# Tiled small matmuls, a turned softmax divisor, and written-out step orders in a decoder layer

## The chip, the core and the metric

The kernel runs on one core of one Trainium2 chip. A core has TensorE (PE in the profile; PEld is its weight load), VectorE (DVE), ScalarE (ACT), GpSimd (POOL) and SyncE (SP, which here only starts DMAs). The metric is the device time of one execution in microseconds. Every engine works through its own instructions in order and waits on semaphores for the others.

## The reference

A decoder layer on 32 rows of 256 tokens with 256 features, all in float32. Three parts, each on a layer norm of `x` and added to `x`:

```python
# part a: gated linear attention, 4 heads, 64 slots
q, k, v = silu(conv4(x @ Wq)), silu(conv4(x @ Wk)), silu(conv4(x @ Wv)); q, k = rope(q, k)
s = clip(x @ Ws, -32, 32); z = cumlogsumexp(s)        # over the tokens
# hk = hk * exp(z_prev - z) + k (x) exp(s - z); ok = q . hk; qv = softmax(ok)
# hv = hv * exp(z_prev - z) + exp(s - z) (x) v; o = qv . hv
x = x + (rmsnorm(o) * gnorm * silu(x @ Wg)) @ Wo
# part x: cross attention to 77 context tokens, 16 heads of 16
Q, K, V = x @ W_q.T, ctx @ W_k.T, ctx @ W_v.T
x = x + (softmax(where(mask, Q K^T / 4, -1e10)) @ V) @ W_proj.T + b_proj
# part f: 8 experts of 64, the best two by x @ gate_w
x = x + sum over the two of softmax(top2) * ((silu(x @ Wu[e]) * (x @ Wv[e])) @ Wo[e])
```

## The kernel before

**Rows and parts.** Each of the 32 rows goes through four stages, one stage an iteration, so four rows are in work at once: `N` (norm and projections of part a, row i), `A` (its attention, row i-1), `X` (cross attention, row i-2), `F` (experts, row i-3). `iterations` runs `body` B + 3 = 35 times; in the first three and the last three some stages are missing and their steps are simply left out. On each engine `body` is one written-out list of steps, and the list is the order in which the engine works. After iteration 0 every engine also runs `others`, in which the second lot of weights is split; PE waits there for all of the splits.

**Precision.** A matrix that needs float32 accuracy is held as two `fp32r` halves and multiplied three times (`mm_halves`). Operands in plain float32 (`AT`, `E`, `vtok`, `q_bd`, `ET`, `probT`, `Vbd`, and all transposes) are multiplied directly, and the profile shows two MATMULs and two LDWEIGHTS for each such call.

**The three places that the change touches in the matmuls.** `a_A` gives k^T q for all four heads at once: `q_bd` holds q of each head in its own 32 partitions and zeros elsewhere, 4 x 256 columns. `a_P` does the same with `qn_bd` (two heads of 64 partitions each, zeros elsewhere). Both use the whole 128 x 128 array, with products by zero in it. `x_av` multiplies the turned probabilities `probT` (stationary, 128 tokens) with the values `Vbd` (moving): for each of 10 tiles of keys and each of two halves of the row, 34 or 51 columns: 16 values and a one per head. The column of ones gives the sum of the exponentials, `x_rs` takes its reciprocal on VectorE, `x_o` multiplies, and `x_ot` turns the result for the projection `x_proj`.

**Scores.** `x_s(u)`, u = 0 to 7, writes four heads' scores into bank X0; `x_soft(u)` (DVE) takes the row maximum, `x_prob(u)` (ACT, four ACTIVATEs) the exponentials; `x_s(u+1)` waits for `x_prob(u)`, since there is one bank. `x_pt(u)` turns two or three tiles of them (PE, then ACT). Bank X0 is also that of `x_turn`, `x_q` and `x_proj`, so row r+1 starts its part x only after `x_out(r)`.

**Context.** K and V of all rows come from 20 matmul groups `g_mm` in iterations 0 to 2, go to memory and come back row by row (`x_kin`, `x_vbd`). `x_kbd` on POOL spreads K over the heads with zeros: four pieces `K_bd` and two of `KT_lo_bd`, all behind the last scores of the row before.

## Time and profile before

| | us |
|---|---|
| median of 3 runs | 1520.54 (1518.21 to 1521.38) |
| profiled execution | 1518.72 |
| its span on the core | 1516.6 |
| PE busy | 1456.9, 96% |
| DVE, ACT, POOL busy | 1217.1, 961.4, 828.6 |

The span is the time from the first to the last instruction; the execution's own time is 2.1 us longer. A busy PE is not PE at its peak: its matmuls overlap, and an entry's length includes the way through the array. What a matmul costs is therefore read from the distance between the starts of two neighbours, not from its length.

### The profile page before, as it was taken

To read this page: it belongs to the slowest core of one execution; us is meant where nothing else is said; L and a number is where in the kernel's file an instruction comes from. 1 tells how busy PE (TensorE), PEld (TensorE's weight loads), DVE (VectorE), ACT (ScalarE), POOL (GpSimd) and SP (SyncE) were. 2 spreads that over 40 slices of the span, in tenths; PEclk is the share of its full clock that TensorE was granted. 3 is DMA by queue.
4 is the path that set the end of the run, shared out by engine and by line. 5 is a ranking of instruction groups with operands and counts; after the bars stand their busy time and mean duration, and the time that the engine had idled before them with its cause. 6 is when DMAs were issued, how large, how long until landed. Compare 5 with 4: busy or idle time off the path is not lost.

```text
span 1516.6 us, 31405 instructions
## 1 busy us (share of the span) xinstructions
PE 1456.9 (96%) x10520; PEld 1291.4 (85%) x10520; DVE 1217.1 (80%) x3006; ACT 961.4 (63%) x2531; POOL 828.6 (55%) x937
## 2 busy tenths in 40 slices
PE   5798999999999999999999999999999999999975
...
DMA packets 113102, 45.03 MB, mean 30 GB/s; under 512 B 86192, under 2 KB 109104, under 8 KB 112944
## 3 DMA queue, kind: packets, MB, share of 16 engines
...
q14 instruction: 72, 0.59, 0.1%
...
## 4 chain that ended last, share of the span: by engine, by line
PE 91%; DVE 3%; issue 2%; POOL 1%; ACT 1%; DMA 1%; SPq 0%; POOLq 0%; DVEq 0%; ACTq 0%
PE bank L444 76%; PE bank L450 7%; PE bank L685 5%; PE bank L770 2%; PE bank L532 1%; DVE a_conv L887 1%; PE bank L738 0%; DVE a_rC L909 0%; ACT x_prob L1331 0%; SPq L433 0%; DMA x_prob<-in_ctxT 0%; DVE x_nmax L1013 0%; DMA x<-in_x 0%; PE bank L541 0%; DVE x L1035 0%
## 5 line engine op out<-in xcount | busy, mean ns | idle before, releaser
L1331 ACT ACTIVATE x_prob<-bank,x_nmax 128x77 f32<-128x77 f32 x1024 | 248.5, 329 | 51.2 <-DVE x_nmax L1013 50.2
L1013 DVE TENSOR_REDUCE x_nmax<-bank 128x4 f32<-128x308 f32 x256 | 120.1, 469 | 109.8 <-PE bank L444 106.0
L1344 ACT ACTIVATE x_probT<-bank 128x256 f32<-128x256 f32 (+1 forms) x256 | 112.2, 438 | 98.3 <-PE bank L685 98.1
L1497 POOL TENSOR_TENSOR a_orinv<-a_ove,mhalf 128x8 f32<-128x8 f32 x32 | 65.1, 2035 | 199.1 <-DVE a_ove L952 199.1
L444 PE MATMUL bank<-x_Vbd,x_probT 128*128 128x34 f32 (+1 forms) x1280 | 162.5, 267 | 0.7 <-DVE x_o L1027 0.7
L887 DVE SCALAR_TENSOR_TENSOR a_conv<-a_raw,cw,a_conv 128x256 f32<-128x256 f32 x384 | 155.0, 478 | 7.5 <-POOL a_conv L1459 7.5
L444 PEld LDWEIGHTS bank<-x_Vbd,x_probT 128*128 128x128 f32 x1280 | 158.0, 192 | 1.1 <-DVE x_o L1027 1.1
L685 PE MATMUL bank<-ident,x_prob 128*128 128x128 f32 x640 | 114.6, 277 | 0.4 <-ACT x_prob L1331 0.3
L909 DVE RECIPROCAL a_rC<-bank 128x512 f32<-128x512 f32 x32 | 107.1, 3348 | 0.6 <-PE bank L444 0.6
L912 DVE TENSOR_TENSOR a_AT<-bank,tri 128x512 f32<-128x512 f32 x128 | 87.7, 685 | 23.9 <-PE bank L444 23.9
L444 PE MATMUL bank<-x_K_bd,x_Q_stack 128*128 128x308 f32 x256 | 94.5, 369 | 8.6 <-ACT x_prob L1331 5.2
L685 PEld LDWEIGHTS bank<-ident,x_prob 128*128 128x128 f32 x640 | 79.5, 145 | 21.9 <-ACT x_prob L1331 9.7
L1450 POOL TENSOR_SCALAR a_E<-a_E 128x512 f32<-128x512 f32 x32 | 62.1, 1940 | 54.9 <-ACT a_E L1230 54.9
L1459 POOL TENSOR_SCALAR a_conv<-a_raw,cw 128x256 f32<-128x256 f32 x128 | 59.1, 479 | 56.3 <-ACT a_raw L1224 56.3
L1535 POOL TENSOR_TENSOR f_s<-f_s,f_wt 128x512 f32<-128x512 f32 x64 | 66.7, 1043 | 39.0 <-DVE f_wt L1098 25.0
L1349 ACT ACTIVATE x_oT_hi<-bank 128x512 fp32r<-128x512 f32 x32 | 19.2, 598 | 107.2 <-PE bank L450 107.2
L1510 POOL TENSOR_TENSOR x_K_bd<-x_K_stack,groupmask 128x308 fp32r<-128x308 f32 x128 | 86.0, 704 | 0.0
L1434 POOL TENSOR_TENSOR x_rstd<-x_ve,mhalf 128x2 f32<-128x2 f32 x32 | 22.9, 715 | 114.6 <-DVE x_neg L842 114.6
L444 PE MATMUL bank<-x_negmask,ident_bf 128*128 128x308 bf16 x256 | 79.6, 311 | 0.0
L444 PE MATMUL bank<-x_KT_lo_bd,x_Q_stack 128*128 128x308 f32 x256 | 77.4, 302 | 0.0
L1513 POOL TENSOR_TENSOR x_KT_lo_bd<-x_KT_lo,headmask 128x616 fp32r<-128x616 f32 x64 | 76.8, 1221 | 0.0
L444 PE MATMUL bank<-fwo_hi,f_sT_hi 128*128 128x256 f32 x256 | 75.2, 294 | 1.5 <-ACT f_sT_hi L1378 1.5
...
## 6 DMA issues: line engine op xcount, KB each, us to landing
...
x_Vbd<-v_tok SPq DMA_DIRECT2D x128, 9.6 KB
```

Source lines behind the costliest of these rows:

```text
L444: return pe.matmul(out, lhsT, rhs, start=start, stop=stop, skip_group_check=True)
L450: ins = pe.transpose(dst[:, k * T + c * P:k * T + (c + 1) * P], src[:, c, k * P:(k + 1) * P], ident[:])
L685: ins = pe.transpose(X1[:, i * P:(i + 1) * P], prob[:, t * P:(t + 1) * P], ident[:])
L887: stt(conv[:, j, :], raw[:, j, i:i + T], cw[:, j, i:i + 1], conv[:, j, :], ALU.mult, ALU.add).then_inc(on.a_conv, 1)
L909: dve.reciprocal(flat(rC[r % 2]), E0[:, :]).then_inc(on.a_rC, 1)
L912: return tt(dst, src.rearrange("p (h t) -> p h t", h=H), tri.rearrange("p (o t) -> p o t", o=1).broadcast_to([P, H, P]), ALU.mult)
L1013: dve.tensor_reduce(nmax[:, u % 2, :], X0[:, 0:UH * S2].rearrange("p (h s) -> p h s", h=UH), AX.X, ALU.min).then_inc(on.x_max, 1)
L1331: ins = act.activation(prob[:, col:col + S2], X0[:, i * S2:(i + 1) * S2], ACT.Exp, scale=-1.0, bias=nmax[:, u % 2, i:i + 1])
L1344: act.activation(probT[:, g[0]:g[-1] + 1, :].rearrange("p h t -> p (h t)"), X1[:, 0:len(g) * P], ACT.Copy).then_inc(on.x_pT, 1)
L1510: pool.tensor_tensor(K_bd[:, q], K_stack[r % 2][:, q:q + 1, :].broadcast_to([P, UH, S2]), spread(groupmask[:], S2), ALU.mult)
L1513: ins = pool.tensor_tensor(KT_lo_bd[:, f], KT_lo[r % 2][:, f:f + 1, :].broadcast_to([P, HB, S2]), spread(headmask[:], S2), ALU.mult)
L1535: pool.tensor_tensor(fs[:, c, :].rearrange("p (e q) -> p e q", e=NE), fs[:, c, :].rearrange("p (e q) -> p e q", e=NE), spread(wt[:, c, :], ...
```

## The change

**Matmul tiles.** `a_A` and `a_P` now multiply 64 partitions at a time (row tiles 0 to 63 and 64 to 127), one tile into bank A0, the other into A1, each with only its own heads. `qn_bd` and `qn_last` become one plain tile `qnT`, filled by one ACTIVATE in place of three; `q_bd` keeps two column blocks in place of four. In `x_av` the sides are swapped: `Vbd` is stationary with 64 columns (four heads of 16), `probT` moves with 256 columns (both halves of the row), and two column tiles write partitions 0 to 63 and 64 to 127 of bank X2. So part x comes out turned already, 12 calls a row in place of 20.

**The divisor.** The ones in `Vbd` are gone. `x_prob` has each exponential give its sum too (`accum_out`, 32 a row). `x_rs` inverts the sums, a new POOL step `x_rse` spreads them over 16 features (two of 128 x 256 a row), `x_rt` turns that (four transposes, where `x_ot` had four), ACT copies it to `rsT`, and `x_on` multiplies on DVE. `x_ot` on ACT copies from `xo` in place of a bank. `x_prob` also waits for `x_rs` of the row before.

**Orders.** `iterations` calls `first()`, `body(i)` for i = 3 to 31, and `last()`: three lists per engine. `x_kbd`, `a_conv`, `a_rc` (the reciprocal of 128 x 512, now two of 128 x 256) and `f_yy` are cut into single steps that the lists place. The splits of the weights are steps (`w_hi_`, `w_lo_`) in `first()`, and each user waits for its own weight only. `Vbd` is zeroed by POOL and no longer loaded.

```diff
@@ PE @@
-            def a_A(r, c):
-                if c == 0:
-                    ...
-                mm((A0 if c == 0 else A1)[:, :], qkr[r % 2][:, 1, c * P:(c + 1) * P],
-                   q_bd[r % 2][:, :, c * P:(c + 1) * P]).then_inc(on.a_A_ps, 1)
+            def a_A(r):
+                ...
+                for c in range(TC):
+                    for i in range(2):
+                        rows = slice(i * P // 2, (i + 1) * P // 2)
+                        ins = mm((A0 if i == 0 else A1)[:, c * D:(c + 1) * D], qkr[r % 2][rows, 1, c * P:(c + 1) * P],
+                                 q_bd[r % 2][rows, :, c * P:(c + 1) * P])
+            def a_P(r):
+                pe.wait_ge(on.a_qnT, upto(r))
+                for c in range(TC):
+                    for f in range(2):
+                        for i in range(2):
+                            rows = slice(i * P // 2, (i + 1) * P // 2)
+                            ins = mm((A1 if i == 0 else A0)[:, c * D + f * P:c * D + (f + 1) * P],
+                                     ET[r % 2][rows, f, c * P:(c + 1) * P], qnT[rows, f, c * P:(c + 1) * P])
+            def x_av(r, g):
+                ...
+                pe.wait_ge(on.x_pT, upto(r, NU, QU + 2 * (g + 1)))
+                for j in range(VS // 2):
+                    for i in range(2):
+                        t = g * NT // 2 + 2 * i + j
+                        ins = mm(X2[i * VW:(i + 1) * VW, g * T:(g + 1) * T], Vbd[r % 2][:, g, i * VS // 2 + j, :],
+                                 probT[:, t, :], start=(j == 0), stop=(j == VS // 2 - 1))
+            def x_rt(r):
+                pe.wait_ge(on.x_rse, upto(r, TC))
+                pe.wait_ge(on.x_pT, upto(r, NU))
+                ...
+                        ins = pe.transpose(X1[:, f * T + c * P:f * T + (c + 1) * P],
+                                           rse[:, c, f * P:(f + 1) * P], ident[:])
@@ DVE @@
-            def x_rs(r, c):
-                dve.wait_ge(on.x_av_ps, upto(r, NU, (c + 1) * QU))
-                ...
-                tt(xo[:, c, :].rearrange("p (h e) -> p h e", h=NH), src[:, :, 0:HD],
-                        spread(xrs[:, c, :], HD), ALU.mult).then_inc(on.x_o, 1)
+            def x_rs(r, c):
+                dve.wait_ge(on.x_prob, upto(r, NU, (c + 1) * QU))
+                ...
+            def x_on(r):
+                dve.wait_ge(on.x_av_ps, upto(r, 2))
+                dve.wait_ge(on.x_rT, upto(r))
+                ...
+                tt(flat(xo), X2[:, :], flat(rsT), ALU.mult).then_inc(on.x_on, 1)
@@ ACT @@
-                                         bias=nmax[:, u % 2, i:i + 1])
+                                         bias=nmax[:, u % 2, i:i + 1], accum_out=xsum[:, c, q * UH + i:q * UH + i + 1])
@@ POOL @@
+            def x_rse(r, c):
+                ...
+                pool.tensor_scalar(rse[:, c, :].rearrange("p (h e) -> p h e", h=NH), spread(xrs[:, c, :], HD),
+                                   1.0, 1.0, ALU.mult, ALU.mult).then_inc(on.x_rse, 1)
@@ orders, PE's list of the body, a line of each @@
-                N(g_mm, 3); X(x_pt, 0); X(x_s, 1); F(f_lg); N(a_v); A(a_qt); X(x_s, 2); F(f_v0); N(a_s)
-                X(x_av, 6); X(x_av, 7); N(a_et); A(a_wo); X(x_ot); F(f_yy); X(x_proj)
+                x_proj(i - 3); a_vtok(i - 1); a_A(i - 1); g_mm(i, 0); x_turn(i - 2); a_state(i - 1)
+                x_pt(i - 2, 0); a_P(i - 1); x_pt(i - 2, 1); x_s(i - 2, 4); x_pt(i - 2, 2); a_o(i - 1)
```

**PE in the middle of the body, before**, from `x_s(3)` on (`x_K_bd`, `x_KT_lo_bd`, `x_negmask` are the three matmuls of a score step, `ident,x_prob` is `x_pt`):

```order
L444 MATMUL bank<-x_K_bd,x_Q_stack 128x308
L444 MATMUL bank<-x_KT_lo_bd,x_Q_stack 128x308
L444 MATMUL bank<-x_negmask,ident_bf 128x308
L444 MATMUL bank<-a_qn_bd,a_ET 128x256 x4
L685 MATMUL bank<-ident,x_prob 128x128 x3
L444 MATMUL bank<-x_Vbd,x_probT 128x34
L444 MATMUL bank<-x_Vbd,x_probT 128x51
L444 MATMUL bank<-x_K_bd,x_Q_stack 128x308
L444 MATMUL bank<-x_KT_lo_bd,x_Q_stack 128x308
L444 MATMUL bank<-x_negmask,ident_bf 128x308
L685 MATMUL bank<-ident,x_prob 128x128 x2
```

The same place after:

```order
L425 MATMUL bank<-x_K_bd,x_Q_stack 128x308
L425 MATMUL bank<-x_KT_lo_bd,x_Q_stack 128x308
L425 MATMUL bank<-x_negmask,ident_bf 128x308
L693 MATMUL bank<-ident,x_prob 128x128 x2
L425 MATMUL bank<-a_qnT,a_ET 128x128 x8
L693 MATMUL bank<-ident,x_prob 128x128 x3
L425 MATMUL bank<-x_K_bd,x_Q_stack 128x308
L425 MATMUL bank<-x_KT_lo_bd,x_Q_stack 128x308
L425 MATMUL bank<-x_negmask,ident_bf 128x308
```

`a_P` (the `a_qn_bd` row, now `a_qnT` with 128 columns) stands between two turns of the probabilities, and no value matmul stands between the score steps any more.

**PE at the end of the body, before** (`ident,f_s` is `f_st(1)`):

```order
L770 MATMUL bank<-ident,f_s 128x128 x4
L685 MATMUL bank<-ident,x_prob 128x128 x3
L444 MATMUL bank<-x_Vbd,x_probT 128x34
L444 MATMUL bank<-x_Vbd,x_probT 128x51
L444 MATMUL bank<-x_Vbd,x_probT 128x34 x2
L444 MATMUL bank<-x_Vbd,x_probT 128x51
L444 MATMUL bank<-x_Vbd,x_probT 128x34
L444 MATMUL bank<-x_Vbd,x_probT 128x51
L444 MATMUL bank<-x_Vbd,x_probT 128x34
L450 MATMUL bank<-ident,a_E 128x128 x4
```

After:

```order
L693 MATMUL bank<-ident,x_prob 128x128 x3
L431 MATMUL bank<-ident,a_o 128x128 x4
L793 MATMUL bank<-ident,f_s 128x128 x4
L425 MATMUL bank<-x_probT,x_Vbd 64x256 x6
L716 MATMUL bank<-ident,x_rse 128x128 x4
L425 MATMUL bank<-wo_hi,a_oT_hi 128x256
```

The row that read 34 and 51 columns is now 6 calls of 256 columns with 64 results each; the first six stand ahead of `a_c`. The turn of the divisor follows.

**DVE at the start of the run, before** (`wo_lo` to `fwo_lo` are the splits of the second lot of weights):

```order
L995 TENSOR_TENSOR f_sT_lo<-bank,f_sT_hi 128x512 x2
L909 RECIPROCAL a_rC<-bank 128x512
L903 SCALAR_TENSOR_TENSOR a_qkv<-a_qkv,a_conv 128x512
L1158 TENSOR_SCALAR x_o<-a_o,gnorm 128x512
L1153 TENSOR_TENSOR wo_lo<-x_o,wo_hi 128x512
L1153 TENSOR_TENSOR xwq_lo<-x_0,xwq_hi 128x512
L1153 TENSOR_TENSOR xwp_lo<-x_1,xwp_hi 128x512
L1153 TENSOR_TENSOR fgate<-f_topf,fgate 128x2x8
L1153 TENSOR_TENSOR fwu_lo<-f_s,fwu_hi 128x512 x2
L1153 TENSOR_TENSOR fwv_lo<-a_E,fwv_hi 128x512
```

After:

```order
L935 SCALAR_TENSOR_TENSOR a_conv<-a_raw,cw,a_conv 128x256 x6
L898 TENSOR_SCALAR a_okn<-a_o,gnorm 128x512
L857 BN_STATS a_stats<-x_1 128x6 x2
L906 TENSOR_TENSOR wo_lo<-a_okn,wo_hi 128x512
L863 BN_AGGR a_mv<-a_stats 128x2 x2
L935 SCALAR_TENSOR_TENSOR a_conv<-a_raw,cw,a_conv 128x256 x6
L941 SCALAR_TENSOR_TENSOR a_qkv<-a_qkv,a_conv 128x512
L926 SCALAR_TENSOR_TENSOR a_gate<-a_gate,bank 128x512
L946 STREAM_SHUFFLE a_conv<-a_qkv 128x512
```

The convolution is cut in two by the step that needs the second lot of weights, and the splits that stood in one piece behind `a_rC` are spread over three rows' steps.

**PE's first rows, before**, where K of the context came first:

```order
L444 MATMUL bank<-x_prob,xwk 128x512 x4
L444 MATMUL bank<-xwv,x_prob 128x256 x4
L450 MATMUL bank<-ident,a_xn 128x128 x4
L444 MATMUL bank<-a_xnT_hi,wqk_hi 128x256
```

After:

```order
L431 MATMUL bank<-ident,a_xn 128x128 x4
L425 MATMUL bank<-a_xnT_hi,wqk_hi 128x256
L425 MATMUL bank<-a_xnT_lo,wqk_hi 128x256
L425 MATMUL bank<-a_xnT_hi,wqk_lo 128x256
L425 MATMUL bank<-a_xnT_hi,wqk_hi 128x256
```

Row 0's transpose and projections are first, and the context waits behind them.

## Rows read from the trace of the kernel before

**Rows 1.** The page's busy line and the sum of its chain that ended last.
```profile
PE 1456.9 (96%) x10520; PEld 1291.4 (85%) x10520; DVE 1217.1 (80%) x3006; ACT 961.4 (63%) x2531; POOL 828.6 (55%) x937
...
PE 91%; DVE 3%; issue 2%; POOL 1%; ACT 1%; DMA 1%; SPq 0%; POOLq 0%; DVEq 0%; ACTq 0%
```

**Rows 2.** Busy us in three stretches: PE, PEld, DVE, ACT, POOL, then clock, DMA.
```profile
0.00:134.00 134.00, 102.43 (x585) 79.45 (x586) 80.29 (x161) 64.14 (x143) 54.01 (x63) 0.97 0.42 129
134.00:1405.00 1271.00, 1270.07 (x9426) 1141.20 (x9425) 1084.43 (x2697) 852.71 (x2264) 746.77 (x842) 1.00 0.09 21
1405.00:1516.60 111.60, 84.37 (x514) 70.70 (x512) 52.38 (x148) 44.55 (x126) 27.82 (x33) 0.88 0.05 13
```

**Rows 3.** The four transposes that open each iteration, from the third on.
```profile
L532 PE MATMUL bank<-ident,a_qkv x120: 270/272/273, 134.0 to 1405.4; 128*128 128x128 f32 x120
```

**Rows 4.** PE in order of time: start us, us, line, out<-in, shapes.
```profile
704.71 1.02 PE L444 MATMUL bank<-a_q_bd,a_qkr 128*128 128x512 f32 x2
705.57 0.60 PE L450 MATMUL bank<-ident,x_xn 128*128 128x128 f32 x4
...
722.84 1.89 PE L444 MATMUL bank<-a_qn_bd,a_ET 128*128 128x256 f32 x8
724.57 0.49 PE L685 MATMUL bank<-ident,x_prob 128*128 128x128 f32 x3
...
739.70 1.87 PE L444 MATMUL bank<-x_Vbd,x_probT 128*128 128x34 f32 x16
741.40 0.64 PE L450 MATMUL bank<-ident,a_E 128*128 128x128 f32 x4
```

**Rows 5.** Weight loads by form: count, busy us and mean ns.
```profile
L444 PEld LDWEIGHTS bank<-f_xnT_hi,fgate 128*16 128x16 f32 x64 | 6.6, 104 | 2.6 <-ACT f_xnT_hi L1354 1.8
...
L738 PEld LDWEIGHTS bank<-ident,f_lgT 16*128 16x128 f32 x64 | 6.3, 135 | 4.9 <-issue 0.6
```

**Rows 6.** PE timeline around the two tile forms that there are.
```profile
714.06 0.30 PE L444 MATMUL bank<-x_KT_lo_bd,x_Q_stack 128*128 128x308 f32 x1
714.20 0.31 PE L444 MATMUL bank<-x_negmask,ident_bf 128*128 128x308 bf16 x1
...
714.46 0.28 PE L444 MATMUL bank<-f_xnT_lo,fgate 128*16 128x256 f32 x1
714.58 0.28 PE L444 MATMUL bank<-f_xnT_hi,fgate 128*16 128x256 f32 x1
...
716.80 0.31 PE L444 MATMUL bank<-x_negmask,ident_bf 128*128 128x308 bf16 x1
...
717.26 0.39 PE L444 MATMUL bank<-a_xnT_hi,wv_hi 128*128 128x256 f32 x1
717.48 0.28 PE L444 MATMUL bank<-a_xnT_lo,wv_hi 128*128 128x256 f32 x1
```

**Rows 7.** ScalarE timeline: four exponentials, and the smallest ACTIVATE.
```profile
717.66 0.97 ACT L1331 ACTIVATE x_prob<-bank,x_nmax 128x77 f32<-128x77 f32 x4 [0.24 <-DVE x_nmax L1013]
718.50 0.22 ACT L1364 ACTIVATE f_egap<-f_gap 128x2 f32<-128x2 f32 x1
```

**Rows 8.** Chain that ended last: one round of scores of the last row.
```profile
1460.84 0.71 PE bank L444 x3
...
1463.11 0.70 PE bank L444 x3
```

**Rows 9.** Start of the run: the first split of a weight on ScalarE.
```profile
L1409 ACT ACTIVATE wqk_hi<-a_AT x1: 629/629/629, 10.0 to 10.0; 128x512 fp32r<-128x512 f32 x1
```

**Rows 10.** PE timeline at the start, with the idle time before an entry.
```profile
13.55 6.19 PE L444 MATMUL bank<-x_prob,xwk 128*128 128x512 f32 x8 [13.55 <-DMA x_prob<-in_ctxT]
...
50.02 1.09 PE L532 MATMUL bank<-ident,a_qkv 128*128 128x128 f32 x4 [6.78 <-DVE fwo_lo L1153]
```

**Rows 11.** Chain that ended last, at the end of the run.
```profile
1448.34 2.64 POOL x_K_bd L1510 x4
```

**Rows 12.** PE timeline at the end.
```profile
1453.58 0.59 PE L444 MATMUL bank<-x_K_bd,x_Q_stack 128*128 128x308 f32 x1 [2.22 <-POOL x_KT_lo_bd L1513]
```

More of the change, by code:

```diff
@@ L140, in build @@
         qkr = [sb(f"a_qkr_{i}", [P, 2, T]) for i in range(2)]
-        q_bd = [sb(f"a_q_bd_{i}", [P, H, T]) for i in range(2)]
+        q_bd = [sb(f"a_q_bd_{i}", [P, 2, T]) for i in range(2)]
         ktok = sb("a_ktok", [P, P])
@@ L275, in build, with iterations @@
         KV_OUT = 16 * 4
-        def row(i):
-            return i if 0 <= i < B else None
-        def iterations(body, others):
-            for i in range(B + 3):
-                body(row(i), row(i - 1), row(i - 2), row(i - 3))
-                if i == 0:
-                    others()
+        def iterations(first, body, last):
+            first()
+            for i in range(3, B):
+                body(i)
+            last()
         block = ctx.enter_context(nc.Block())
@@ L809, in others @@
[L809 to L819 removed]
+                mm_halves(F0[:, c * D:(c + 1) * D], [
+                    (lambda h, i=i: fsT[h][:, c, i, :], lambda h, i=i: fwo[h][:, i, :]) for i in range(RC)]
+                    ).then_inc(on.f_y_ps, 1)
@@ new lines, in first @@
+            def first():
+                a_turn(0); a_qk(0); g_mm(0, 0); a_v(0); g_mm(0, 1); g_mm(0, 2); a_s(0); g_mm(0, 3)
+                a_g(0); g_mm(0, 4); g_mm(0, 5); g_mm(0, 6); a_c(0); g_mm(0, 7); g_mm(1, 0); a_ktok(0)
+                a_et(0); a_A(0); a_vtok(0); g_mm(1, 1); a_state(0); a_turn(1); a_ok(0); a_qk(1)
+                g_mm(1, 2); a_v(1); a_qt(0); a_P(0); a_s(1); a_o(0); g_mm(1, 3); a_g(1); g_mm(1, 4)
+                g_mm(1, 5); a_ot(0); g_mm(1, 6); a_wo(0); a_c(1); g_mm(1, 7); g_mm(2, 0); g_mm(2, 1)
+                x_turn(0); g_mm(2, 2); a_et(1); a_ktok(1); a_vtok(1); a_A(1); x_q(0); a_turn(2)
+                g_mm(2, 3); a_qk(2); x_s(0, 0); a_state(1); a_v(2); x_pt(0, 0); x_s(0, 1); a_ok(1)
+                x_s(0, 2); x_pt(0, 1); a_s(2); x_pt(0, 2); x_s(0, 3); a_qt(1); x_s(0, 4); x_pt(0, 3)
+                a_P(1); a_g(2); x_s(0, 5); a_o(1); x_s(0, 6); x_pt(0, 4); x_pt(0, 5); a_c(2); x_s(0, 7)
+                x_pt(0, 6); x_av(0, 0); x_pt(0, 7); a_ot(1); x_av(0, 1); x_rt(0); a_wo(1); a_et(2)
+                a_ktok(2)
@@ L822, in _ @@
+            iterations(first, body, last)
         @block.vector
@@ L1166, in _ @@
             dve.tensor_copy(ones_r[:], ones[:])
-            dve.wait_ge(ld_w, W_LANDED)
-            dve.tensor_copy(tri_r[:], tri_raw).then_inc(w_ready, 1)
-            dve.tensor_copy(ident_bf[:], ident[:]).then_inc(w_ready, 1)
-            split(splits, 0)
-            dve.wait_ge(w_ready, 4)
-            iterations(body, others)
+            iterations(first, body, last)
         @block.scalar
@@ L1422, in _ @@
+            iterations(first, body, last)
         @block.gpsimd
@@ L1562, in _ @@
                 pool.memset(q_bd[i][:], 0.0).then_inc(z_ready, 1)
-            pool.memset(qn_bd[:], 0.0).then_inc(z_ready, 1)
-            def others():
-                pool.wait_ge(ld_v, V_LANDED)
-                pool.wait_ge(on.g_ps, 4)
-                pool.memset(prob[:], 0.0).then_inc(z_ready, 1)
-                pool.wait_ge(z_ready, 4)
-            pool.wait_ge(ld_w, W_LANDED)
-            pool.wait_ge(w_ready, 4)
-            iterations(body, others)
+            for i in range(2):
+                pool.memset(Vbd[i][:], 0.0).then_inc(v_zero, 1)
+            iterations(first, body, last)
 def constants():
```

602 lines of the change are left out of this document (348 added, 254 removed).

## Prediction, made before the run

> **What bounds the kernel now.** I read the page's sums first, then the chain that ended last, then busy time by stretch, then PE's timeline inside one iteration. The sums show PE busy for 96% of the span and 91% of the chain on PE [rows 1]. The stretches show where that holds: from 134 to 1405 us PE is busy 1270.07 of 1271.00 us at full clock, while DVE has 1084.43, ACT 852.71 and POOL 746.77 us of it [rows 2]. The first 134 us have 102.4 us of PE and the last 111.6 us have 84.4 [rows 2]. So the middle is bound by what PE issues, the two ends by dependencies. The transposes that open an iteration start at 134.0 for iteration 3 and at about 1405.1 for iteration 32 (the last of four is at 1405.4) [rows 3]: 29 iterations in 1271.1 us, 43.83 us each. Per iteration DVE has 1084.43 / 29 = 37.4, ACT 29.4 and POOL 25.8 us. The span is 134.0 + 1271.1 + 111.5 = 1516.6 us.
>
> **x_av.** A row has 20 calls before, that is 40 matmul passes (float32 takes two). Sixteen of them run from 739.70 to 741.40, 106 ns each [rows 4], though they have only 34 or 51 columns: the load of 128 weight columns sets that pace. 40 x 0.106 = 4.25 us. After there are 12 calls, 24 passes of 256 columns. Eight passes of 256 columns take 722.84 to 724.57, 0.216 us each [rows 4]. One after the other that is 5.19 us, 0.94 more than before. If the two column tiles always ran beside each other it would be half, 2.60. As written, each call's two passes come in a row, so only the second pass of a call can lie beside the first of its neighbour: 7 slots for 12 passes, 14 x 0.216 = 3.02 us. No row has two tiles in flight, so 2.60 and 5.19 are the bounds; I take 3.02, saving 1.22, since the two tiles of a pair share neither partitions of the bank nor columns of the array. The loads shrink with the columns (104 ns for 16 columns against 135 ns for 128, the latter with only 16 partitions [rows 5]), so 64 columns don't bind 216 ns passes.
>
> **a_A.** Two calls of 512 columns before, 704.71 to 705.57 for one [rows 4]: 1.72 us. After, four calls of 256, eight passes: 1.73 in single file, 0.86 fully paired, 5 slots or 1.08 as written. I take 1.08, saving 0.64.
>
> **a_P.** 1.73 us before (722.84 to 724.57 [rows 4]). After, 16 passes of 128 columns, each with its own load of 128 columns. A load doesn't get shorter with fewer partitions [rows 5], and 16 loads at the 106 ns of rows 4 are 1.70 us; if the loads of two row tiles run beside each other it is 9 slots of 0.108, 0.97 us as written and 0.86 at best. Neither row decides between them; I take the middle, 1.35, saving 0.38. The three together save 2.24 us a row, between a loss of 0.94 and a gain of 3.4.
>
> **Switches of the tile form.** An iteration gets four such places (`a_A`, `a_P`, two `x_av`), eight changes of form. The trace has two places like them. Into the 16-column form: 714.20 to 714.46 for a pass of 308 and one of 256 columns, 0.26 us, exactly the 0.14 (714.06 to 714.20) and 0.12 (714.46 to 714.58) that they take anyway [rows 6]. Into and out of the 16-partition form: from 716.80 to 717.48 stand a 0.14, two small transposes of 0.11, and a 0.12, 0.48 in all, and 0.68 passes: 0.10 a change [rows 6]. So between 0 and 0.8 us an iteration; I take 0.4. Here a rule speaks against the change: the Trainium skill, "TensorEngine Tiling (Array Packing)", section Key Properties, says that a change of tiling mode drains the engine. By rows 4 the way through the array is 1.89 - 1.73 = 0.16 us, so by the rule the eight changes are 1.3 us and the total comes out 26 us higher than mine. Rows 6 speak against a full drain, at least for the column form.
>
> **The sums on ACT.** The 32 exponentials of a row now give their sum. Four take 0.97 us with 0.33 for the last, a pitch of 0.21; the smallest ACTIVATE lasts 0.22 [rows 7], of which the same overlap of 0.12 hides a part. Bounds: 0 and 0.22 each; I take 0.10, as if a small instruction were put behind each. That is 3.3 us of ACT an iteration, while three ACTIVATEs of `a_qnt` become one (about -1 us) and `x_rt` adds 0.6: 29.4 becomes 32.3 of some 42, hidden. POOL gets two spreads of 256 elements; like-sized POOL work is 0.5 to 1 us each, so 27 us, hidden. DVE loses 0.3 us (one multiplication in place of two). What isn't hidden is the round of scores: PE, DVE, ACT and PE again take 1460.84 to 1463.11, 2.27 us [rows 8]; with four sums 2.69. The next score step stands behind a round's wait in PE's queue, and everything of PE behind it. In the new body the shortest distances have between two score steps 12 projection passes and four transposes, or `a_P` and five transposes, with the step itself about 2.5 us. So PE waits some 0.2 us at two of them: 0.3 us an iteration. If a sum costs nothing it is 0; at 0.22 each the round is 3.15 and five of the seven gaps are short by about 0.5, 2.5 us.
>
> **Moved work in the body.** `x_proj` opens it and `x_turn` still waits for `x_out`, with four transposes, `a_A` and nothing in `g_mm` from row 3 on between: 0.44 + 1.08 us cover DVE's 0.7. The cut reciprocal lets a_otl and f_stl pass between its halves. Nothing of DVE or SP becomes the last to end there; cost nil, cover 5 us of DVE time an iteration.
>
> Per iteration: -2.24 + 0.4 + 0.3 = -1.54; x 29 = -44.7 us.
>
> **Start.** PE starts at 13.55, waiting for the context, and stands idle 6.78 us before 50.02 for the splits of the second lot [rows 10]. The first lot of weights has landed by 10.0 [rows 9]. After, row 0's transposes can go at 10, so the chain of row 0 starts some 10 us earlier than behind eight cold K passes, and the splits fall between steps. The new order has its own gap: the first step that needs the second lot stands in the middle of row 0's convolution, and holds DVE and the gate behind it, at worst as long as the old wait. Of 134 - 102.4 = 31.6 us without PE I take back 12, and the tiles of rows 0 and 1 give 3: -15, bounds 0 and -28.
>
> **End.** The last row's scores waited for POOL's K pieces, 1448.34 to 1453.58, with PE idle [rows 11, 12]; they are now placed singly. The tiles of three rows' steps give 3. The last 33 us (experts of row 31) keep their order. -10, bounds 0 and -18.
>
> Sum: -44.7 - 15 - 10 = -70 on 1516.6, span 1447; the execution is 2.1 us above its span, so 1449. The median of the runs shown is 1.8 above the profiled execution, hence **1451 us**.
>
> **Rivals.**
> All tiles side by side, loads too: `x_av` 2.60, `a_A` and `a_P` 0.86, 3.4 us saved an iteration less 0.2, x 29 = -93; with -28 at the ends 1400 us. For it: tiles in different partitions share nothing in the array. Against: the passes are issued in the order written. The same page and section of the Trainium skill says that tiles can load and multiply in parallel; this case's trace doesn't show it.
> The score round takes PE's place as the bound: 2.5 us of waits in place of 0.3, +64 on mine with the ends somewhat slower: 1510 at its worst, 1490 for half of it. For it: every gap between score steps has become shorter by the value matmuls that left. Against: ACT and DVE each keep 5 to 10 us of an iteration free.
> The ends give nothing: 1476. Against: 27 us of end idle have named causes.
> Slower: the tiles run in single file. Place: `x_av`. 24 passes of 0.216 replace 40 of 0.106, +0.94 us, `a_A` and `a_P` save nothing, the switches cost 0.4 to 0.8: +1.5 an iteration, +44; with half of my end gains, 1520.5 + 44 - 12 = 1552; with all of them 1540. It decides once the saving of the pairing is under 0.5 us an iteration. For it: no row shows two matmuls beside each other.
>
> **How the numbers follow.** Mine 0.50; side by side 0.18; score round 0.14; ends give nothing 0.09; single file 0.09. The first four are faster, less 0.01 each for about no change and slower where the score round is at its worst. 0.2% is about what a measurement of this kernel can tell from no change. Faster 0.88, same 0.02, slower 0.10. The range reaches from just under the side-by-side case, 1398, to the score round's 1496; it leaves out single file and the worst of the score round.
>
> **What would show it.** Distance between starts of `a_vtok`'s transposes about 42.3 us. Starts in `x_av`: pairs under 20 ns apart with 0.21 between pairs; single file shows 0.21 throughout. `a_P`'s 16 passes over 1.0 (loads side by side) or 1.7 us. ACT's exponentials: pitch 0.31 in place of 0.21. PE idle behind `x_prob` in the middle: 0.3 us an iteration, 2 if the score round binds. Row 0's first transpose at about 10 us and iteration 3 opening at about 119. I am wrong if the iteration stays above 43, or the first stretch above 130.

## The result and the profile after

The changed kernel takes 1486.56 us (median of 4 runs, 1485.8 to 1488.57) against 1519.38 us for the kernel before on the same chip (4 runs): ratio 0.978, 95% interval 0.976 to 0.979. It is 32.8 us faster. I had forecast 1451 us, so the direction was right and more than half of the gain is missing. The page of the changed kernel's profile has these sums, the chain that ended last by engine, and ACT's two groups of exponentials and sums (count | busy us, mean ns | idle before):

```profile
PE 1406.1 (95%) x10392; PEld 1197.1 (81%) x10392; DVE 1205.7 (81%) x3006; ACT 1035.4 (70%) x3523; POOL 862.4 (58%) x1002
...
PE 66%; DVE 19%; issue 5%; ACT 4%; SPq 3%; POOL 1%; DMA 1%; POOLq 0%; ACTq 0%; DVEq 0%
...
L1416 ACT ACTIVATE x_prob<-bank,x_nmax 128x77 f32<-128x77 f32 x1024 | 318.7, 327 | 145.9 <-DVE x_nmax L1069 143.3
L1416 ACT ACTIVATION_READ_ACCUMULATOR x_prob<-bank,x_nmax 128x1 f32 x1024 | 210.3, 205 | 0.0
```

PE lost 51 us of work against [rows 1], but its share of the chain fell from 91% to 66%, and DVE now has 19% of it. Each exponential with a sum has become two instructions. Next, the opening transposes of `a_vtok` for rows 2 and 31 on PE (start, duration), the rows that answer to [rows 3], and busy time by stretch between them, as in [rows 2]:

```profile
125.81 0.60 PE L529 MATMUL bank<-ident,a_qkv 128*128 128x128 f32 x4
...
1377.43 0.60 PE L529 MATMUL bank<-ident,a_qkv 128*128 128x128 f32 x4
```

```profile
core 0: us, PE busy (x) PEld busy (x) DVE busy (x) ACT busy (x) POOL busy (x), PEclk, DMA share, GB/s
0.00:126.00 126.00, 100.74 (x595) 78.45 (x596) 80.48 (x165) 65.27 (x172) 56.84 (x66) 0.97 0.45 136
126.00:1377.40 1251.40, 1224.68 (x9321) 1056.67 (x9320) 1075.09 (x2702) 920.62 (x3163) 777.41 (x901) 1.00 0.09 21
1377.40:1486.80 109.40, 80.68 (x480) 61.97 (x478) 50.12 (x141) 49.55 (x188) 28.12 (x36) 0.90 0.04 11
```

29 iterations take 1251.6 us, 43.16 each where 43.83 were and 42.29 were forecast. PE is idle for 26.7 us of the middle (0.92 an iteration), before it was 0.93 us in all. The start gave 8.1 us (forecast 15), the end 2.1 (forecast 10). The span is 39.8 us above the 1447 of my sum (my terms add up to 1446.9): 25.1 in the middle, 6.9 at the start, 7.9 at the end.

**The tiles.** PE in the changed kernel, around `a_P` and the first half of `x_av`:

```profile
704.76 0.38 PE L693 MATMUL bank<-ident,x_prob 128*128 128x128 f32 x2
705.07 1.16 PE L425 MATMUL bank<-a_qnT,a_ET 64*128 64x128 f32 x16
706.16 0.55 PE L693 MATMUL bank<-ident,x_prob 128*128 128x128 f32 x3
...
716.82 0.38 PE L693 MATMUL bank<-ident,x_prob 128*128 128x128 f32 x2
717.13 1.52 PE L425 MATMUL bank<-x_probT,x_Vbd 128*64 128x256 f32 x12
718.57 0.38 PE L425 MATMUL bank<-a_Er_hi,tri 128*128 128x256 f32 x1
718.80 0.28 PE L425 MATMUL bank<-a_Er_lo,tri 128*128 128x256 f32 x1
```

Sixteen passes of `a_P` take 1.09 us, where one file of them is 16 x 0.108 = 1.73 and perfect pairs are 0.86; twelve of `x_av` take 1.44, between 2.59 and 1.30. So the passes lie beside each other nearly without exception, loads too, and what is above the perfect pairs sits at the borders. There the loads (PEld) show why:

```profile
705.07 0.97 PEld L425 LDWEIGHTS bank<-a_qnT,a_ET 64*128 64x128 f32 x16 [0.17 <-issue]
...
717.13 1.06 PEld L425 LDWEIGHTS bank<-x_probT,x_Vbd 128*64 128x64 f32 x12 [0.17 <-issue]
718.57 0.19 PEld L425 LDWEIGHTS bank<-a_Er_hi,tri 128*128 128x128 f32 x1 [0.38 <-issue]
```

No load is pulled ahead over such a border. Two transposes take 0.22, so the 0.31 ahead of 705.07 hold 0.09 of gap; 1.09 - 0.86 = 0.23 are at the end of `a_P`. For `x_av` it is 0.09 ahead, 1.44 - 1.30 = 0.14 at the end and 0.23 - 0.12 = 0.11 after the next pass, 0.34 in all. The four places of an iteration sum to about 1.2 us.

**The seam.** PE where the iteration opens (the idle time in brackets stands before the row), and DVE there:

```profile
685.60 0.60 PE L529 MATMUL bank<-ident,a_qkv 128*128 128x128 f32 x4
686.12 1.13 PE L425 MATMUL bank<-a_q_bd,a_qkr 64*128 64x256 f32 x8
687.34 0.63 PE L431 MATMUL bank<-ident,x_xn 128*128 128x128 f32 x4
688.65 0.67 PE L425 MATMUL bank<-a_E,a_ktok 128*128 128x256 f32 x2 [0.69 <-DVE a_AT L962]
...
689.67 0.36 PE L425 MATMUL bank<-x_xnT_hi,xwq_hi 128*128 128x256 f32 x1
```

```profile
685.51 0.74 DVE L857 BATCH_NORM_STATS2 a_stats<-x 128x6 f32<-128x256 f32 x2
...
686.46 0.66 DVE L1091 TENSOR_TENSOR x<-bank,x 128x512 f32<-128x512 f32 x1
...
687.17 0.75 DVE L857 BATCH_NORM_STATS2 f_stats<-x 128x6 f32<-128x256 f32 x2
687.83 0.67 DVE L962 TENSOR_TENSOR a_AT<-bank,tri 128x512 f32<-128x512 f32 x1
```

`a_state` writes the bank that the first mask (`a_AT`) reads. `a_A` is over at about 687.2, but DVE works without a pause through this stretch and masks from 687.83 to 688.5. PE waits 0.69 us, 29 times (19.7 us). By the starts it loses more: from `x_turn` to `a_state` it is 688.65 - 687.34 = 1.31 us, where four transposes take 0.44, so 0.87. Before, the second call of `a_A` (0.86 us) stood between `x_turn` and `a_state` and covered it. Two more such waits are filed under "issue": `f_gate` and `a_qk` follow the low halves of their inputs by a tenth of a microsecond. PEld and DVE in the changed kernel, then PEld at the same place in the kernel before:

```profile
694.55 0.10 PEld L425 LDWEIGHTS bank<-x_negmask,ident_bf 128*128 128x128 bf16 x1
694.85 0.09 PEld L425 LDWEIGHTS bank<-f_xnT_hi,fgate 128*16 128x16 f32 x1 [0.20 <-issue]
...
695.49 0.19 PEld L425 LDWEIGHTS bank<-a_xnT_hi,wqk_hi 128*128 128x128 f32 x1 [0.28 <-issue]
```

```profile
694.09 0.69 DVE L884 TENSOR_TENSOR f_xnT_lo<-bank,f_xnT_hi 128x512 fp32r<-128x512 f32 x1
694.69 0.68 DVE L884 TENSOR_TENSOR a_xnT_lo<-bank,a_xnT_hi 128x512 fp32r<-128x512 f32 x1
```

```profile
670.33 0.10 PEld L444 LDWEIGHTS bank<-x_negmask,ident_bf 128*128 128x128 bf16 x1
670.34 0.11 PEld L444 LDWEIGHTS bank<-f_xnT_hi,fgate 128*16 128x16 f32 x1
```

Before, the 16-column load followed without a gap (its form costs nothing); after, it comes 0.3 us later, when `f_xnT_lo` is there. The pass ahead takes 0.14, so PE loses 0.18 here and 0.17 at `a_qk`. That these two are waits for the low halves is read from the times; no run tested it.

### The profile page after: what moved, and what is told of

It reads as the page before. It is cut to its first block, busy times and chain, and to the rows that moved or that the text cites. A ratio compares the mean times of both kernels' runs of the same rounds, so it can differ in the third digit from the quotient of the medians.

```text
span 1486.8 us, 32816 instructions
## 1 busy us (share of the span) xinstructions
PE 1406.1 (95%) x10392; PEld 1197.1 (81%) x10392; DVE 1205.7 (81%) x3006; ACT 1035.4 (70%) x3523; POOL 862.4 (58%) x1002
## 4 chain that ended last, share of the span: by engine, by line
PE 66%; DVE 19%; issue 5%; ACT 4%; SPq 3%; POOL 1%; DMA 1%; POOLq 0%; ACTq 0%; DVEq 0%
PE bank L425 56%; PE bank L431 4%; PE bank L693 3%; ACT x_prob L1416 3%; PE bank L793 2%; DVE x_o L1084 1%; DVE a_rC L959 1%; DVE x_stats L857 1%; DVE x L1091 1%; DVE f_stats L857 1%; DVE a_stats L857 1%; DVE x_nmax L1069 1%; DVE x_oT_lo L884 1%; DVE a_AT L962 1%; DVE x L1023 1%
## 5 line engine op out<-in xcount | busy, mean ns | idle before, releaser
L1416 ACT ACTIVATE x_prob<-bank,x_nmax 128x77 f32<-128x77 f32 x1024 | 318.7, 327 | 145.9 <-DVE x_nmax L1069 143.3
L1416 ACT ACTIVATION_READ_ACCUMULATOR x_prob<-bank,x_nmax 128x1 f32 x1024 | 210.3, 205 | 0.0
L1650 POOL TENSOR_TENSOR f_s<-f_s,f_wt 128x512 f32<-128x512 f32 x64 | 77.7, 1215 | 152.2 <-DVE f_wt L1154 114.7
L935 DVE SCALAR_TENSOR_TENSOR a_conv<-a_raw,cw,a_conv 128x256 f32<-128x256 f32 x384 | 165.6, 492 | 0.0
L959 DVE RECIPROCAL a_rC<-bank 128x256 f32<-128x256 f32 x64 | 111.6, 1746 | 1.2 <-PE bank L425 1.1
L425 PE MATMUL bank<-x_probT,x_Vbd 128*64 128x256 f32 x768 | 97.0, 388 | 0.0
L962 DVE TENSOR_TENSOR a_AT<-bank,tri 128x512 f32<-128x512 f32 x128 | 84.6, 682 | 12.4 <-PE bank L425 12.2
L1594 POOL TENSOR_TENSOR a_okn<-a_okn,a_okmax 128x512 f32<-128x512 f32 x32 | 33.6, 1050 | 89.5 <-DVE a_okmax L984 89.5
L1058 DVE SCALAR_TENSOR_TENSOR x_Q_stack<-bank,x_Q_stack 64x512 fp32r<-64x512 f32 x64 | 44.1, 688 | 51.0 <-ACT x_Q_stack L1399 50.5
L1602 POOL TENSOR_TENSOR a_orinv<-a_ove,mhalf 128x8 f32<-128x8 f32 x32 | 53.4, 1670 | 43.3 <-DVE a_ove L1006 43.3
```

The costliest lines, as they stand in the source:

```text
L425: return pe.matmul(out, lhsT, rhs, start=start, stop=stop, skip_group_check=True)
L935: stt(conv[:, j, :], raw[:, j, i:i + T], cw[:, j, i:i + 1], conv[:, j, :], ALU.mult, ALU.add).then_inc(on.a_conv, 1)
L959: dve.reciprocal(rC[r % 2][:, c, :], E0[:, c * D:(c + 1) * D]).then_inc(on.a_rC, 1)
L962: return tt(dst, src.rearrange("p (h t) -> p h t", h=H), tri.rearrange("p (o t) -> p o t", o=1).broadcast_to([P, H, P]), ALU.mult)
L1416: ins = act.activation(prob[:, col:col + S2], X0[:, i * S2:(i + 1) * S2], ACT.Exp, scale=-1.0, bias=nmax[:, u % 2, i:i + 1], accum_out=xsu ...
L1650: pool.tensor_tensor(fs[:, c, :].rearrange("p (e q) -> p e q", e=NE), fs[:, c, :].rearrange("p (e q) -> p e q", e=NE), spread(wt[:, c, :], ...
```

## The experiments

All ran against the kernel before on the same chip; unless said otherwise each is the changed kernel with the edit shown. The table has the median, the start of row 2's `a_vtok` (start), the mean iteration from there to row 31's, and the rest of the span (end). The last three columns come from the profiled execution of each. The kernel before had medians of 1518.9 to 1521.2 us beside these runs, so a difference of one or two us between rows is not read.

| kernel | us | ratio to before (95%) | start | iteration | end |
|---|---|---|---|---|---|
| before | 1519.4 | | 133.95 | 43.83 | 111.5 |
| changed | 1486.6 | 0.976 to 0.979 | 125.81 | 43.16 | 109.4 |
| no sums | 1474.3 | 0.969 to 0.972 | 124.93 | 42.79 | 107.3 |
| output late | 1496.9 | 0.984 to 0.986 | 124.28 | 43.51 | 109.4 |
| tiles apart | 1522.5 | 1.001 to 1.004 | 129.15 | 44.27 | 110.4 |
| values together | 1514.9 | 0.995 to 0.998 | 125.36 | 44.11 | 108.6 |
| input sums later | 1509.2 | 0.992 to 0.994 | 123.00 | 44.01 | 107.9 |
| seam reordered | 1507.5 | 0.991 to 0.993 | 123.34 | 43.81 | 109.9 |
| a_P split | 1506.0 | 0.990 to 0.993 | 123.62 | 43.86 | 109.3 |
| a_A whole | 1488.7 | 0.978 to 0.981 | 126.05 | 43.24 | 109.3 |
| third input | 1482.9 | 0.974 to 0.977 | 123.92 | 43.12 | 106.8 |
| third, output late | 1489.8 | 0.979 to 0.983 | 123.28 | 43.30 | 107.8 |
| third, low half on POOL | 1486.1 | 0.976 to 0.980 | 123.77 | 43.19 | 107.8 |
| x_av split | 1486.8 | 0.976 to 0.980 | 124.57 | 43.19 | 108.4 |
| third, silu on POOL | 1478.3 | 0.972 to 0.974 | 124.57 | 42.91 | 109.4 |
| the same, no sums | 1475.3 | 0.969 to 0.972 | 126.22 | 42.82 | 108.4 |
| before with sums | 1542.1 | 1.014 to 1.017 | 135.82 | 44.57 | 117.2 |
| silu on POOL, x_av split | 1487.7 | 0.978 to 0.981 | 124.75 | 43.22 | 107.8 |
| convolution first | 1488.2 | 0.977 to 0.981 | 124.53 | 43.17 | 106.4 |
| all three edits | 1479.5 | 0.971 to 0.974 | 125.50 | 42.91 | 108.3 |

**No sums.**

```
-  bias=nmax[:, u % 2, i:i + 1], accum_out=xsum[...])
+  bias=nmax[:, u % 2, i:i + 1])        # and xsum set to 1 once
```

> The changed kernel (1486.6 us) without the sums on ACT: the exponentials no longer accumulate and the reciprocals are taken of a constant 1, so the softmax is not normalised. Theory A (the seam): the middle is held at 43.15 us by DVE's queue where two iterations meet, PE waits 0.69 us there for the mask, and the sums cost only what PE waits behind x_prob: 0.04 us an iteration by the trace, up to 0.4 if the exposed loads behind it count, and 0.37 us in each of some 8 bare score rounds at the end: 1474 to 1482 us. Theory B (the sums): four reads of 0.2 us lengthen every score round, and that took 1 us an iteration of the gain: 1450 to 1458 us.

It fell in theory A's range, at its lower end; the softmax is not normalised here. The sums cost 0.37 us an iteration and 3 us at the ends. What PE still waits for between 130 and 1370 us starts with

```profile
PE bank L425 <- DVE a_AT L962: 10.3, 28, 0.7
```

where the changed kernel has 19.2 us, 28 times. So most of what the sums cost in the middle, 8.9 of some 10.4 us, is part of the wait for the mask and not a second loss beside it; behind `x_prob` itself PE waited 1.1 us in all of the changed kernel's middle.

**Output late.** `f_out(i - 3)` leaves the end of body i; `f_out(i - 4)` stands behind `a_maskA(i - 1, 0)`.

> Only DVE's order is changed: the output addition f_out of row i-3 goes from the end of body i to behind the first mask of body i+1. Theory A: everything of DVE at the seam comes 0.6 us earlier, so the first mask ends at 2.3 instead of 2.9 us after the iteration's first transpose and PE's 0.69 us wait in front of a_state falls to 0.1; the next thing, x_q, then waits 0.3 for x_xnT_lo. Gain 0.3 to 0.6 us an iteration: 1469 to 1478 us. Theory B: DVE's order has no part in it, within 1 us of 1486.6.

Neither: it lost 10 us. PE still waits 0.45 us for the mask and another 0.5 for `x_xnT_lo`, which now stood behind `f_out`. The chain that ended last shows what holds the mask (start, length, what):

```profile
728.38 0.61 DVE x L1023
...
729.01 2.65 DMA x<-in_x
...
731.68 0.43 DVE a_stats L857
```

`a_out` frees the buffer into which the input of the row after next is loaded, and `a_stats` waits for that load. In the changed kernel `a_out` ends at 682.5, the load some 2.65 us later, and DVE comes to `a_stats` at 685.51: a second path through the seam lay 0.3 us behind DVE's queue.

**Tiles apart.** In `a_A`, `a_P` and `x_av` the loop over the tile `i` goes outermost.

```
-  for j in range(VS // 2):
-      for i in range(2):
+  for i in range(2):
+      for j in range(VS // 2):
```

> The same matmuls as in the changed kernel, but all calls of one tile before all of the other in a_A, a_P and each half of x_av. If passes lie beside each other only when neighbours in PE's order name different tiles, then nearly all now run in single file: x_av 5.2 instead of 2.6 us of passes, a_A and a_P 1.73 instead of 0.86 each: +4.3 us an iteration at most (less where one pass meets the other tile at the turn: 4 turns of one pass, -0.8), and the 0.9 us of idle may take up some: 1575 to 1620 us. If PE pairs tiles whatever the order: within 3 us of 1486.6.

Neither number: 36 us slower, not 90 to 130. PE at a half of `x_av`, and at `a_A`:

```profile
691.42 2.00 PE L425 MATMUL bank<-x_probT,x_Vbd 128*64 128x256 f32 x12
693.34 0.38 PE L425 MATMUL bank<-a_Er_hi,tri 128*128 128x256 f32 x1
```

```profile
660.33 1.14 PE L425 MATMUL bank<-a_q_bd,a_qkr 64*128 64x256 f32 x8
661.41 0.66 PE L431 MATMUL bank<-ident,x_xn 128*128 128x128 f32 x4
```

Half of `x_av` takes 1.92 us in place of 1.44, `a_P` 1.64 in place of 1.09, and `a_A`, four passes on one tile and then four on the other, 1.08; its entry is 1.14 us long, 1.13 in the changed kernel (there 1.22 to the next start, since `x_turn` comes late). So passes up to some four places apart in the order still run beside each other; with six or eight on one tile only a part of them does (single file would be 2.59 and 1.73).

**Values together.** `x_av(i - 2, 0)` goes from its place ahead of `a_c` to directly ahead of `x_av(i - 2, 1)`.

> Only PE's order is changed: the first half of x_av stands directly ahead of the second, so an iteration has six changes of tile form in place of eight. Theory C (a change of form empties the engine): the trace shows 0.09 us ahead of x_av and 0.14 and 0.11 behind it, so two changes less are worth 0.3 us an iteration: 1477 to 1479 us. If a change costs what I predicted (0.05): 1484 to 1486 us. If instead the seam alone decides, what is saved ahead of it still counts, because the chain into the seam starts from x_av's end.

28 us slower, outside both ranges: the half had been the cover of the last round of scores. PE's waits in the middle (us in total, times, longest):

```profile
PE bank L693 <- ACT x_prob L1416: 37.6, 28, 1.4
```

So it says nothing on the price of a change of form; it shows what a round costs uncovered.

**Input sums later, seam reordered.** DVE's body opens `x_out; a_stats; a_maskA(0); a_mv; a_ve; f_stats; x_xntl; f_mv; f_ve`; the second also swaps `f_turn` with `a_ok`, `f_gate` with `a_qk` on PE and `a_xntl` with `f_xntl` on DVE.

> Only DVE's order at the start of the body is changed: x_out first, then a_stats, the first mask, a_mv, a_ve, f_stats, x_xntl, f_mv, f_ve. Theory A (the seam), mended after the last four runs: DVE works without a pause from the end of x_av to the mask, and a second path, a_out to the load of the next input (2.6 us) to a_stats, ends only 0.3 us earlier; so the work that must go ahead of the mask has to shrink and a_stats must not come earlier. Here f_stats (0.65 us) no longer stands ahead of the mask and a_stats comes later: PE's wait for the mask falls from 0.69 to about 0.1 us, and 0.3 to 0.6 us an iteration are gained, 1468 to 1478 us. Rival: f_xn and a_xn, now up to 0.7 and 1.3 us later, stop PE at a_turn and f_turn instead, 1484 to 1490 us.

> As the last, and PE takes f_turn behind a_ok and f_gate behind a_qk, DVE a_xntl ahead of f_xntl, so that the later f_xn has cover. Theory A: 0.5 to 0.7 us an iteration gained, 1465 to 1472 us, and less than the last one's time if f_turn stopped PE there. Rival (the seam isn't what holds the iteration): within 3 us of 1486.6.

They came out 23 and 21 us slower. The mask's wait fell (8.4 and 5.7 us in all), but PE waited 15.6 us for `x_xnT_lo` in both, and 14.2 for `f_xn` in the first, 10.3 for `x_Q_stack` in the second. The rival of the first named a right wait, `f_xn`, but its 1484 to 1490 us were 19 too low, and both theories of the second missed. At the seam everything of DVE is wanted within a microsecond, and a change of order only picks who is late.

**a_P split, x_av split.** One more pair of form changes each: `a_P(c=0); x_pt(1); a_P(c=1)`, and `x_av(0) j=0,1; a_c; x_av(0) j=2`.

> The same work, but the three transposes x_pt(1) stand between the two halves of a_P, so an iteration has ten changes of tile form in place of eight. Theory C (each change empties the array): 0.3 us more an iteration, less what the 0.92 us of idle absorbs, 1490 to 1496 us. At the 0.05 us a change that I predicted: 1488 to 1490 us.

> The last four passes of the first half of x_av stand behind a_c instead of ahead of it, where nothing waits for them; so ten changes of tile form an iteration and no other difference. In the run that split a_P one more pair cost 0.37 us on PE, but the mask behind it was late too. Theory C: 0.3 to 0.37 us an iteration, 1495 to 1498 us. At my 0.05 a change: 1488 to 1490 us.

The first lost 19 us, but 16 of it are a wait for the mask of `a_P`, 0.55 us ahead of `a_o` in each iteration, so it can't price the pair. The second cost nothing. PE there:

```profile
717.32 0.39 PE L425 MATMUL bank<-a_Er_hi,tri 128*128 128x256 f32 x1
...
718.02 0.28 PE L425 MATMUL bank<-a_Er_lo,tri 128*128 128x256 f32 x1
718.23 0.65 PE L425 MATMUL bank<-x_probT,x_Vbd 128*64 128x256 f32 x4
718.81 0.55 PE L693 MATMUL bank<-ident,x_prob 128*128 128x128 f32 x3
```

Against the changed kernel, PE stands 0.31 us ahead on the way into this stretch and level with it behind: the pair costs 0.31 us, and the seam's waits (the mask's 0.69 fell to 0.42, and `x_turn` came 0.15 earlier) paid for it. Both expectations failed on the time, yet 0.31 a pair is the price that theory C had.

**a_A whole.** Full-height `a_A` in two calls with `x_turn` between, as before the change (the queries' buffer single).

> a_A goes back to the form it had before the change (full height, block-diagonal queries, two calls with x_turn between them, masks one by one; the queries' buffer is single for want of room), all else as changed. By the tiles alone this loses: the passes take 0.86 us more, two changes of form less give back 0.4, so +0.4 us an iteration, 1496 to 1500 us. Theory A: the second call again covers the mask, the 0.69 us wait in front of a_state goes, and the iteration comes out 0.1 to 0.4 us shorter than the changed kernel's: 1475 to 1484 us.

1488.7, between the two: the wait in front of `a_state` is gone, and the passes take back what it cost. The row tiles of `a_A` are worth 2 us in this order, not the 19 of my 0.64 an iteration.

**Third input buffer, alone and with four other edits.** `x0` gets three buffers and `a_load(r)` waits for `a_out(r - 3)`.

> A third buffer for the input rows, so that a load no longer waits for a_out of the row but one before, 2.6 us plus queueing ahead of a_stats. Nothing else is changed. In the changed kernel the load ends 0.3 us before DVE gets to a_stats, so on its own this should do nothing: 1484 to 1488 us. If the load is what holds the iteration together with DVE: 1475 to 1480 us.

> The third input buffer, and f_out behind the first mask of the next body, as in the run that lost 10 us. There the chain of waits went through a_out, the load of x and a_stats. If that load was what failed it, the third buffer turns the loss into a gain: the mask comes 0.6 us earlier and PE waits 0.3 us for x_xnT_lo instead, 1474 to 1482 us. If the loss came from f_out standing ahead of x_xntl: 1493 to 1498 us again.

> The third input buffer, and the low half of x_o's split (0.6 us of DVE at the seam) is taken by POOL, which stands idle there for 2.7 us. No order of another instruction changes. Theory A (DVE's work at the seam holds the iteration): everything of DVE behind it comes 0.6 us earlier, PE's 0.69 us wait for the mask falls to 0.1 and x_q waits 0.2 to 0.3: 0.3 to 0.5 us an iteration, 1471 to 1479 us. If the seam doesn't hold the iteration: 1484 to 1489 us. POOL's subtraction takes 1.3 us against 0.6, so x_proj could wait up to 0.1.

Alone it gains 3.6 us, mostly at start and end, between its two ranges. With `f_out` late it takes 1489.8, again between the two: the late output costs 6.9 us with the third buffer and 10.4 without, so the load was about a third of that loss, and PE still waits 14.1 us for `x_xnT_lo`. With the low half of `x_o` on POOL the time, 1486.1, lies in the range I had set for a seam that doesn't hold the iteration. The trace has another reason: the mask's wait is halved and `x_q` starts 0.2 us sooner after the opening, but POOL took 1.60 us where DVE takes 0.69, and `x_proj` began 0.4 us late. Against the third buffer alone that is 3.2 us lost.

**silu on POOL, and with it: no sums, x_av split.** `a_silu_v` leaves DVE:

```
+  pool.tensor_scalar(v, v, 1.0, 1.0, ALU.add, ALU.mult)
+  pool.tensor_tensor(v, v, conv_v, ALU.mult)     # v, conv_v: the values' half of qkv and conv; waits left out
```

> The third input buffer, and a_silu_v (0.6 us of DVE at the seam) done on POOL in two operations of 0.9 and 1.3 us, where POOL is idle and a_vtok needs it 1 us later. Theory A (DVE's work at the seam holds the iteration): the mask comes 0.5 us earlier, then x_xnT_lo is the next to be late, 0.3 us an iteration less than the 43.12 of the third buffer alone: 1472 to 1477 us. If the iteration is held by PE's own passes and form changes: within 2 us of 1482.9.

> The last kernel without the sums on ACT (the softmax is not normalised, as in the first of these runs). If seam and sums are two separate losses they add up: another 0.3 to 0.4 us an iteration and 2 us at the ends, 1459 to 1466 us. If the sums only lost time through the seam, they are worth little once it is relieved: 1469 to 1475 us.

> The kernel with a_silu_v on POOL, and the last four passes of x_av's first half behind a_c: one more pair of form changes. Alone that put 0.31 us on PE and took 0.31 from its wait for the mask, nothing on the time. With the mask's wait gone there is nothing to take it from: 0.2 to 0.35 us an iteration, 6 to 10 us above e13. If it is again within 2 us of e13, PE's passes don't hold the iteration there either.

Moving 0.6 us of covered DVE work gains 0.21 us an iteration, 1478.3 us, a microsecond outside the range; PE still waits (0.57 us for the mask), since `x_q` can't start until `x_turn`, ACT's copy and `x_xnT_lo` have gone by (3.84 us after the opening; 4.07 in the rows of the changed kernel above, 4.0 on average, never under 3.75 in any). So of the 0.69 us only about 0.3 could be had. Without the sums it gains another 0.09 an iteration, not 0.37, as expected if the two losses overlap. And the pair of form changes that was free now costs 0.31 an iteration, 9.5 us, as expected.

**Before with sums.** The kernel before, `accum_out` added, the sums not used.

> The kernel before with the sums accumulated and not used, 32 a row. PE never waits there, and each round of scores is covered by more passes. If a sum costs only where a round of scores has no cover: 0 to 0.1 us an iteration and 1 to 3 us at the end, 1520 to 1526 us. If it costs 0.39 us an iteration whatever the order: 1530 to 1536 us.

Dearer than either: 23 us by the medians, of which 0.74 us an iteration (21 us) lie in the middle. The 5.7 at the end come from a profiled execution that took 1547.3, 5 us above the median, and may be too high by that. Its first transposes `x_pt(0)` stand directly behind `x_s(0)`'s round and ahead of `x_s(1)`, and there PE now falls 0.35 us behind, at a later `x_pt` another 0.21. The changed order has `x_pt(0)` behind `x_s(3)`.

**Convolution first, and all three edits.** `w_wo`, `a_stats(1)` and the split of Wo go behind row 0's convolution, silu, gate and rotation.

> In the first iterations the scaling of Wo, its split and the input sums of row 1 stand behind row 0's convolution, silu, gate and rotation on DVE (and the split's high half behind a_ehi on ACT), so the wait for the second lot of weights holds none of them. If that gap is the missing part of the start's gain: a_c of row 0 starts 3 to 4 us earlier than 37.0, and the time falls by as much, 1482 to 1484 us. If the start is held by SP's stores and loads of K and V: PE only waits elsewhere, 1485 to 1488 us.

> Third input buffer, a_silu_v on POOL and the start's edit of the last kernel. If the three add up: 1474 to 1476 us; if the start's edit is worth nothing: 1477 to 1480 us.

The wait for the second lot went, row 0's `a_vtok` came at 40.15 in place of 45.69, and 4.3 of these 5.5 us were lost again by row 1's. PE in the changed kernel, then in this one:

```profile
37.01 0.55 PE L425 MATMUL bank<-a_Er_hi,tri 128*128 128x256 f32 x1 [3.82 <-POOL a_Er_lo L1569]
...
45.69 0.63 PE L529 MATMUL bank<-ident,a_qkv 128*128 128x128 f32 x4
```

```profile
40.15 0.66 PE L529 MATMUL bank<-ident,a_qkv 128*128 128x128 f32 x4
...
54.35 0.66 PE L431 MATMUL bank<-ident,a_qn 128*128 128x128 f32 x4 [3.04 <-POOL a_qn L1598]
```

In POOL's queue `a_qn` stands behind the first K pieces, and these wait for K to be written out and read back. POOL stands idle for 10.06 us ahead of the first of them. The time did not change, and added to the kernel with silu on POOL the edit did nothing either. The fastest that normalises its softmax, 1478.3 us, is the one with the third buffer and the silu on POOL: 8 us under the changed kernel.

## Why the prediction was too fast

**The signs.** I had written that I am wrong if the iteration stays above 43; it is 43.16. The first stretch, 125.8, stayed under the 130 that I had named beside it.

**Tiles: near in the net, wrong in both parts.** I had 2.24 us saved and 0.4 lost to changes of form. The passes are paired to the full, 1.65 + 0.86 + 0.87 = 3.38 us, and the changes cost about 1.2. Net 2.2 against my 1.84, near by luck: the two errors cancel in part. "Only the second pass of a call can lie beside the first of its neighbour" failed (tiles apart). For the eight changes I had weighed 1.3 us, by the way through the array [rows 4], and taken 0.4; they cost some 1.2, and 0.31 for a pair. The trace agrees here with the Trainium skill, "TensorEngine Tiling (Array Packing)", Key Properties, that a change of tiling mode drains the engine. [Rows 6] misled me: the 16-column form is not one that changes anything.

**Sums on ACT: right in size, wrong in the place.** A read takes 0.19 to 0.24 us, and the pitch is 0.30 us per exponential with its sum (I had 0.31); ACT in the last row's scores, then PE's bare rounds at the end:

```profile
1425.76 0.33 ACT L1416 ACTIVATE x_prob<-bank,x_nmax 128x77 f32<-128x77 f32 x1 [2.27 <-DVE x_nmax L1069]
1425.99 0.19 ACT L1416 ACTIVATION_READ_ACCUMULATOR x_prob<-bank,x_nmax 128x1 f32 x1
1426.08 0.32 ACT L1416 ACTIVATE x_prob<-bank,x_nmax 128x77 f32<-128x77 f32 x1
```

```profile
1437.43 0.41 PE L425 MATMUL bank<-x_K_bd,x_Q_stack 128*128 128x308 f32 x1 [0.22 <-ACT x_prob L1416]
...
1440.08 0.41 PE L425 MATMUL bank<-x_K_bd,x_Q_stack 128*128 128x308 f32 x1 [1.67 <-ACT x_prob L1416]
```

The round is 2.65 us where [rows 8] had 2.27 and I had 2.69. The 0.3 us an iteration measured 0.37, but that is luck: I had put it behind `x_prob`, 0.2 us at two score steps, and PE waits there for 1.1 us in 29 iterations. The cost comes at the mask (no sums), for which my sum had nothing. By which step the sums delay the mask no run shows. The rival of the score round was also added up wrongly: 1451 + 64 is 1515 before any slower end, not 1510.

**Moved work in the body: the step that failed.** I wrote that nothing of DVE becomes the last to end, with 0.44 + 1.08 us of PE as cover for `x_out`. I checked `x_turn`, which waits for `x_out`, and not `a_state`, which waits for the mask behind it. When `a_A` became one call, the mask lost 0.86 us of cover; that wait is 0.69 us, with 0.35 more at `f_gate` and `a_qk`. The tiles as measured give 43.83 - 2.2 = 41.6; the 43.16 measured leaves 1.5 us, where I had 0.3 for the sums and nothing for this step. The mask takes 0.87 of it by the starts and the other two waits 0.35, 1.2 us; the last 0.3 are spread over the iteration and not located. The sums' 0.37 is no term beside these, since it sits mostly in the mask's wait. With the second call of `a_A` back in its place (a_A whole) that wait was gone, which confirms the cover; but no run took the wait away and kept the tiles. Order edits of DVE at that place all lost; of two edits that took work off DVE there one won 0.21 us an iteration and one nothing; and the rest of the mask's wait hides a second latency of `x_q`. That the order as a whole can't do better is not shown.

**Start.** Row 0's first transposes went at 9.79 as forecast, row 2 came 8.1 us earlier, not 15. The gap at the second lot was there as described, but closing it gives nothing. PE then waits for `a_qn` behind the K pieces, and POOL for K's way out and back; that this way holds the start is read from the trace, and no run shortened it.

**End.** The wait for the K pieces [rows 11, 12] went, and another took its place. PE:

```profile
1421.42 0.60 PE L431 MATMUL bank<-ident,f_xn 128*128 128x128 f32 x4
1424.39 0.38 PE L425 MATMUL bank<-x_K_bd,x_Q_stack 128*128 128x308 f32 x1 [2.38 <-issue]
```

From `x_out` of row 30 (1417.00) to these scores it is 7.4 us, before it was 1453.58 - 1445.25 = 8.3: the queries' own way (`x_turn`, `x_q`, ACT and DVE filling `Q_stack` until 1424.3) was only 0.9 us shorter than the K pieces'. The rounds that follow are each 0.4 us longer. I had named the wait that goes and not the next one.
